# The output projection of an attention layer in fp16 parts, with half of its tiles moved into and behind the attention's units

## What is computed

```python
x = x + attention(layernorm(x))          # w_q, w_k, w_v, softmax(q k^T / 4) v, then w_o
x = x + ffn(layernorm(x))

def ffn(x):
    xq = int4_quant(x)                   # round(x*sqrt7/mean|x|), clipped to -8..7
    gate = bitlinear(xq, w_gate)         # weights rounded to -1, 0, 1 by their mean |w|
    up = bitlinear(xq, w_up)
    inter = int8_quant(up * relu(gate)**2)
    return bitlinear(inter, w_down)      # 512 -> 1376 -> 512
```

## Time and profile before

| | us |
|---|---|
| median of 3 runs (967.86 to 973.85) | 969.07 |
| the profiled execution, its time | 970.29 |
| its span, first to last instruction | 968.5 |
| PE busy / DVE busy / ACT busy / POOL busy in it | 919.0 / 851.1 / 772.3 / 140.1 |

### The profile page before, as it was taken

One profiled execution on the slowest core, in us unless ns is written; L12 is line 12 of the kernel. 1 busy time (PEld: TensorE's weight loads), 2 busy tenths in 40 slices (PEclk: granted clock), 3 DMA queues, 4 the chain that ended last, 5 costly groups with the idle time before them and its releaser, 6 DMA issues.

```text
span 968.5 us, 16815 instructions
## 1 busy us (share of the span) xinstructions
PE 919.0 (95%) x5934; PEld 300.9 (31%) x5934; DVE 851.1 (88%) x1513; ACT 772.3 (80%) x1437; POOL 140.1 (14%) x286
## 2 busy tenths in 40 slices
PE   4898999999999999999999999999898999999985
PEld 3333222222222222222222222222112245555542
DVE  7898899999999999999999999999877177877773
ACT  5653498999899998899998999898785877777773
POOL 3411011121111211112111121110002011112100
PEclk9999999999999999999999999999788999999997
DMA  9720021021121113102112111316540033111000
GB/s 353 228 90 1 0 71 41 24 56 51 50 56 40 40 35 80 41 23 57 54 47 55 40 42 37 78 40 178 185 104 12 12 130 111 45 44 55 22 24 32
DMA packets 38010, 64.92 MB, mean 67 GB/s; under 512 B 3622, under 2 KB 18982, under 8 KB 37670
## 3 DMA queue, kind: packets, MB, share of 16 engines
q1 hardware_dynamic: 37926, 63.85, 22.3%
HBM read 42.27 MB, written 21.23 MB: 66 GB/s over the span
## 4 chain that ended last, share of the span: by engine, by line
PE 80%; DVE 5%; ACT 4%; issue 2%; DMA 1%; SPq 1%; POOL 0%; ACTq 0%; POOLq 0%; DVEq 0%
PE ps L410 25%; PE ps L390 14%; PE ps L354 13%; PE ps L332 8%; PE ps L580 6%; PE ps L549 6%; PE ps L605 3%; DVE mx L1007 3%; PE ps L296 2%; DMA qk<-att_d 1%; ACT PB L744 1%; PE ps L371 1%; PE ps L595 1%; DVE hm L1103 1%; ACT XV L804 1%
## 5 line engine op out<-in xcount | busy, mean ns | idle before, releaser
L1007 DVE TENSOR_REDUCE mx<-ps 128x1 f32<-128x512 f32 x1024 | 632.5, 683 | 24.5 <-PE ps L354 18.1
L744 ACT ACTIVATE PB<-ps 128x512 f32<-128x512 f32 x1024 | 542.7, 597 | 77.0 <-PE ps L390 76.3
L354 PE MATMUL ps<-QK 48*128 48x512 f16 x1024 | 306.1, 388 | 9.3 <-DVE mx L1007 5.3
L390 PE MATMUL ps<-QK 50*128 50x512 f16 x1024 | 297.1, 388 | 3.5 <-ACT PB L744 2.5
L410 PE MATMUL ps<-PB,Vg 128*32 128x512 f32 x2048 | 278.1, 616 | 0.2 <-ACT PB L744 0.2
L390 PEld LDWEIGHTS ps<-QK 50*128 50x128 f16 x1024 | 70.9, 94 | 205.1 <-ACT PB L744 166.6
L354 PEld LDWEIGHTS ps<-QK 48*128 48x128 f16 x1024 | 76.0, 94 | 181.7 <-DVE mx L1007 152.2
L332 PE MATMUL ps<-XV,wqk 128*128 128x512 f16 x384 | 102.5, 385 | 0.0
L1282 POOL TENSOR_SCALAR nmb<-nm 128x16 f16<-128x16 f32 x32 | 6.5, 203 | 543.5 <-DVE nm L1012 543.5
L549 PE MATMUL ps<-wo,XV 128*128 128x512 f32 x128 | 63.1, 621 | 3.0 <-POOL XV L1327 3.0
L410 PEld LDWEIGHTS ps<-PB,Vg 128*32 128x32 f32 x2048 | 40.6, 108 | 69.6 <-ACT PB L744 36.8
(11 more groups left out here) (133 smaller groups left out, 652.6 us busy)
## 6 DMA issues: line engine op xcount, KB each, us to landing
parts_d<-spl SPq DMA_DIRECT2D x64, 128.0 KB
att_d<-OS SPq DMA_DIRECT2D x32, 256.0 KB
QK<-parts_d SPq DMA_DIRECT2D x48, 128.0 KB, 3.9
QK<-parts_d SPq DMA_DIRECT2D x16, 256.0 KB, 4.5
XV<-att_d SPq DMA_DIRECT2D x2, 2048.0 KB, 12.0
wqk<-x SPq DMA_DIRECT2D x16, 256.0 KB, 3.6
QK<-rden_d SPq DMA_DIRECT2D x8, 512.0 KB, 7.9
out<-PB SPq DMA_DIRECT2D x16, 256.0 KB, 2.0
```

The source lines that it names most:

```text
L354: nc.tensor.matmul(ps[:, at % S_BANKS, :], QK[rows, sup % 2, 2 * set_ + p, 0, half * HALF + qt * P:half * HALF + (qt + 1) * P], QK[rows, s ...
L390: nc.tensor.matmul(ps[:, T_BANK + n % T_BANKS, :], QK[rows, sup % 2, 2 * set_ + p, 1, kt * P:(kt + 1) * P], QK[rows, sup % 2, 2 * set_ + p ...
L744: nc.scalar.activation(PB[:, at % 3, i, :], ps[:, T_BANK + n % T_BANKS, :], ACT.Exp, scale=exp_reg).then_inc(probs, 1)
L1007: nc.vector.tensor_reduce(mx[:, v % 2, idx, kh:kh + 1], ps[:, at % S_BANKS, :], AX.X, ALU.max).then_inc(s_used, 1)
```

## The change

The output projection is done in fp16 parts: w_o is scaled by a power of two and split in a high and a low fp16 part, and so is the quotient `att`; a tile is then 12 fp16 matmuls (high x high, high x low, low x high, for four blocks of 128 channels) in place of 4 fp32 ones. Its weight parts lie in `wo`, its raw weights in the not yet used space of the down weights `td`.

- Tiles 0 to 3 are projected in units 26 to 29, in the places of a job. ACT copies the sum with its scale (`act_out_copy`), and POOL adds x (`pool_residual`). Tiles 4 to 7 are projected in the ramp, three matmuls in each step. Tiles 8 to 15 stay in the tail, in the same places (`pe_tile` 4 to 11); tiles 0 to 3 of the tail carry none.
- `pool_att` becomes three operations: product in fp32, cast, difference.
- Added inside the attention: denominators in and w_o in at unit 18 (SP), reciprocals of batch 0 at unit 19 (DVE; before: unit 28), quotients in at units 20 to 23 (SP; before: units 27 and 29), sum of squares of w_o at unit 20 (ACT), its spread over partitions, root and scales at unit 21 (PE, POOL, DVE), high part at unit 22 (ACT), low part at unit 23 (DVE).
- The down weights come in at units 27 and 28, their absolute sums are after steps 2, 10, 17 and 20 of the last super, the mean at step 22, and the rounding after the first two tiles' quantisation, in the ramp.
- The first gate and up chunk of tile 0 stands ahead of the last values' matmul. The scale of the value copies is a constant (two small DVE operations less at the start).

The core of the diff:

```diff
-            if step == RAMP:
-                pe.wait_ge(s_used, SUP_ITEMS * SUPERS)
-                pe_mean(pe, 2)
-            pe_attention_out(pe, (step - RAMP) // 4, step % 4)
             pe_scoresT(pe, sup, step, 0)
             pe_scoresT(pe, sup, step, 1)
             pe_av(pe, sup * STEPS + step - 2)
...
             pe_scoresT(pe, sup, step, 2)
             pe_scoresT(pe, sup, step, 3)
-            if step == 25:
+            if step == RAMP:
+                pe.wait_ge(s_used, SUP_ITEMS * SUPERS)
+            if step == RAMP + 6:
+                pe_mean(pe, 2)
+            n = step - RAMP
+            for m in range(3):
+                pe_attention_out(pe, UNIT_TILES + n // 4, n % 4 * 3 + m)
+            if step == RAMP + 9:
                 pe_xq_transpose(pe, 0)
...
                 def job(*pieces):
-                    if job_in(at):
-                        for m in pieces:
+                    for m in pieces:
+                        if job_in(at):
                             pe_job(pe, job_in(at), m)
+                        elif at >= FIRST_OUT:
+                            pe_attention_out(pe, at - FIRST_OUT, m)
...
                     scores(9)
+                    if at == 21:
+                        pe_norm(pe, 3)
                     if at + 1 < UNITS:
                         pe_max_rows(pe, at + 1)
...
+        def pe_attention_out(pe, t, m):
+
+            k, (a, b) = m // 3, PRODUCTS[m % 3]
+            if m == 0:
                 pe.wait_ge(att_ready, t + 1)
                 if t == 0:
-                    pe.wait_ge(wo_in, 64)
-                elif t == 1:
-                    pe.wait_ge(w_fac, 3)
-                elif t == 3:
+                    pe.wait_ge(wo_low, 1)
+                if t < UNIT_TILES:
+                    pe.wait_ge(rows_used, FIRST_OUT + t + 2)
+                elif t == BT - 1:
                     pe.wait_ge(xq_copy_dve, 1)
-                else:
-                    pe.wait_ge(x2_ready, t - 1 if t <= O_AHEAD else t)
-            last = nc.tensor.matmul(ps[:, o_bank(t), :], att[:, t % 2, g, :], wo[:, g, :],
-                                    start=(g == 0), stop=(g == SPB - 1))
-            if g == SPB - 1:
+                elif t >= UNIT_TILES + 2:
+                    pe.wait_ge(x2_ready, t - UNIT_TILES - (1 if t <= BT else 0))
+            last = nc.tensor.matmul(ps[:, o_bank(t), :], att[:, t % 2, a, k * P:(k + 1) * P], wop[:, b, k, :],
+                                    start=(m == 0), stop=(m == 3 * KT - 1))
...
+                if (at, r) == (20, 4):
+                    act_squares(act, 3)
+                if (at, r) == (22, 4):
+                    act_weights(act, 3, 0, HID)
+                if last and step in (2, 10, 17, 20):
+                    act_abs_down(act, (2, 10, 17, 20).index(step))
...
-                if n == (SUPERS - 1) * SUP_ITEMS + AHEAD + 7:
+                if n == 19 * UNIT_ITEMS + AHEAD + 16:
                     dve_reciprocal(dve, 0)
+                elif n == 21 * UNIT_ITEMS + AHEAD + 9:
+                    dve_total_squares(dve, 3)
+                elif n == 21 * UNIT_ITEMS + AHEAD + 22:
+                    dve_scales(dve, 3)
+                    dve_out_scale(dve)
+                elif n == 23 * UNIT_ITEMS + AHEAD + 4:
+                    dve_weights(dve, 3, 0, HID, 6)
...
         def pool_att(pool, t):
...
-            nc.gpsimd.tensor_tensor(att[:, t % 2, :, :], num[b][:, :, at:at + P], rdn[:, b, :, at:at + P], ALU.mult)\
-                .then_inc(att_ready, 1)
+            w = att32[b]
+            nc.gpsimd.tensor_tensor(w.rearrange("p (g t) -> p g t", g=SPB), num[b][:, :, at:at + P], rdn[b][:, :, at:at + P], ALU.mult)\
+                .then_inc(att_step, 1)
+            own_wait(pool, att_step, 2 * t + 1)
+            cast(att[:, t % 2, 0, :], w).then_inc(att_step, 1)
+            own_wait(pool, att_step, 2 * t + 2)
+            nc.gpsimd.tensor_tensor(att[:, t % 2, 1, :], w, att[:, t % 2, 0, :], ALU.subtract).then_inc(att_ready, 1)
```

More of the change, by code:

```diff
@@ L570, in pe_gate_up @@
                     pe.wait_ge(x2_ready, 2)
-                    for w in range(3):
+                    for w in range(2):
                         pe.wait_ge(w_tern[w], 4)
+                    pe.wait_ge(probs, 4 * UNITS * KEYT - 2)
                 else:
@@ L620, in pe_tile @@
                 pe_xq_transpose(pe, t + 1)
-            if t + O_AHEAD < TILES:
-                for g in range(SPB):
-                    pe_attention_out(pe, t + O_AHEAD, g)
+            if BT <= t + O_AHEAD < TILES:
+                for m in range(3 * KT):
+                    pe_attention_out(pe, t + O_AHEAD, m)
             if t >= 1:
@@ L719, in act_abs, with act_abs_down, act_out_copy @@
         def act_abs(act, w, q):
-            if wsum_first(w, q):
-                act.wait_ge(raw_in[w // 2], 16 * (4 + w // 2))
-                if w == 2:
-                    act.wait_ge(down_zero, 1)
+            if wsum_first(w, q) and w == 0:
+                act.wait_ge(gate_in, 16 * 4)
             nc.scalar.activation(ternq(w, q), raw(w, q), ACT.Abs, accum_out=wsum[:, w, q:q + 1]).then_inc(w_abs[w], 1)
+        def act_abs_down(act, q):
+            act.wait_ge(down_in[q // 2], (32, 48)[q // 2])
+            if q == 0:
+                for r in range(2):
+                    act.wait_ge(parts_out[r], 32 * 2 * SUPERS)
+            else:
+                act.wait_ge(w_abs[2], q)
+            if q == 2:
+                act.wait_ge(down_zero, 1)
+            nc.scalar.activation(spl[:, :, :, :].rearrange("p s a n -> p (s a n)").bitcast(BF16)[:, 0:DQ], raw(2, q), ACT.Abs,
+                                 accum_out=wsum[:, 2, q:q + 1]).then_inc(w_abs[2], 1)
+        def act_out_copy(act, t):
+            act.wait_ge(o_psum, t + 1)
+            if t == 0:
+                act.wait_ge(os_ready, 1)
+                act.wait_ge(job_split, JOBS)
+            elif t >= 2:
+                act.wait_ge(x2_pool, t - 1)
+            nc.scalar.activation(qk32[:, t % 2, :], ps[:, o_bank(t), :], ACT.Copy, scale=oscale[:, 1:2]).then_inc(o_copy, 1)
         def act_sign(act, w, q, order):
@@ L769, in act_superunit @@
                         act_rows(act, at + 1)
-                if last and step in (4, 6, 8, 10):
-                    act_abs(act, 2, (step - 4) // 2)
+                if (at, r) == (20, 4):
[4 more added lines that the diff above has]
+                    act_abs_down(act, (2, 10, 17, 20).index(step))
             if last:
@@ L1148, in dve_early_tiles @@
                     dve_quant(dve, 0)
+            dve_x2(dve, UNIT_TILES)
+            dve_total(dve, 2)
+            dve_factor(dve, 2)
+            for q in range(4):
+                dve_round(dve, 2, q, q)
+                if q == 3:
+                    dve.wait_ge(att_ready, BT)
+                dve_ternary(dve, 2, q, q)
+            nc.vector.tensor_scalar(wfd[:], wfac[:, 2:3], 1.0 / 127.0, None, ALU.mult)
             dve_xq_copy(dve, 0)
-            dve_x2(dve, 2)
-            dve_x2(dve, 3)
+            for t in range(UNIT_TILES + 1, BT):
+                dve_x2(dve, t)
         def dve_tile(dve, t):
```

261 lines of the change are left out of this document (154 added, 107 removed).

## The result

The changed kernel takes 956.96 us, the median of four runs (955.78 to 960.85), where the kernel before took 968.47 beside it (965.51 to 973.85): a ratio of 0.9882, 95% interval 0.9848 to 0.9917, so 1.2% faster, 11.5 us between the medians. In a later set of six runs it took 955.78 (953.36 to 958.41) against 969.71, a recorded ratio of 0.9839, interval 0.981 to 0.9869, and 13.9 us between the medians. One of the 17 runs of the kernel before in that set took 2120.3 us and doesn't count in the ratio. The profiled run of the first set is its slowest, 960.85 us with a span of 959.1; its stretches are cut at the places where the earlier trace rows cut those of before.

What follows compares the result with a forecast made beforehand. PE was taken to bound units with a job, DVE those without, 0.16 us apart. Costs of 8.1, 3.4 and 0.6 and gains of 10.2, 10.6, 0.6 and 10.0 sum to -19.3 from 970.3: 951 us, range 943 to 962.

Steps and rivals of the forecast that it cites:

- Inserted in units 19 to 23, 8.1 + 3.4: Units 19 to 23: moved reciprocals and w_o preparation cost 8.1 us, one 6.83 us stretch of half clock another 3.4.
- Units 26 and 27, +0.6: Units 26 and 27: becoming job units costs 2 x 0.16 us, the first quotient's close timing 0.3.
- rival D: Units 26 to 31: quotients or factors come late and PE stands, 1.5 us in unit 26, up to 5 in ramp; 957, chance 0.12.
- Units 28 and 29, -10.2: Mark of unit 28 to last joining: 44.91 us falls to 33.49 plus 1.2, without reciprocals or clock falls.
- two absolute sums behind which PE, now full, waits 0.6 each: Units 28 and 29: PE's waits behind ACT's sums of the down weights add 1.2 us.
- The ramp, -10.6: Ramp: 3.7 us gap and half clock (3.4) go, fp16 matmuls save 5.0, less 1.5 for ACT; step 2.70 to 2.39.
- the first chunk, -0.6: End of the ramp: tile 0's earlier gate and up chunk fills the wait for the last exponentials, saving 0.6 us.
- The tail, -10.0: Tail, maximum 0 to 15: 158.0 us against 167.98; projection tiles 10.46 in place of 11.37.
- the reciprocals of batch 1 stay there: Start of the tail: the first two tiles take 22.0 us, against 22.72 before.
- clock 1.00 from unit 26 on: From unit 26 on: a sign to look for, full granted clock of 1.00.
- A: Units 19 to 23: no clock fall (-3.4 us), banks hide more, insertions cost 5.5; 945, chance 0.18.
- B: Tail: POOL slows one DVE operation by 1.1 us in each of eight projection tiles, +8.9 us; 960, chance 0.10.

Runs made afterwards that it cites:

- experiment 8: Changed kernel with the four absolute sums of the down weights on DVE behind the first two tiles' moments instead of on ACT; median 953.84 us.
- experiment 1: Changed kernel with w_o's high part (ACT) and low part (DVE) each cut into four pieces; median 955.23 us.
- experiment 4: Changed kernel with w_o's squares, high part and low part over 8 columns in place of 512, the rest left out; median 949.83 us.
- experiment 3: Changed kernel with each of ACT's four absolute sums of the down weights over 64 columns in place of 1408; median 954.49 us.
- experiment 10: Kernel before the change with unit 28's batch 0 reciprocals over 8 of 256 columns; median 967.05 us against 969.71, ratio 0.997.
- experiment 2: Changed kernel without eleven of the twelve projection matmuls of each of the four tiles in units 26 to 29; median 957.29 us.
- experiment 11: Changed kernel with the batch 0 reciprocals made a second time, in unit 28, result unused; median 956.98 us.
- experiment 6: Changed kernel with tile 0's first gate and up chunk back behind the last attention matmuls; median 958.69 us.
- experiment 7: Changed kernel with ACT's first gate ahead of the copy of the last sums, and batch 1's reciprocal at the end of tile 1; median 957.76 us.
- experiment 5: Changed kernel without the third of the three fp16 products in the ramp and the tail; median 953.26 us.
- 9: Changed kernel with w_o's parts in pieces, absolute sums on DVE and first chunk back behind the last attention matmuls; median 952.13 us, ratio to before 0.9803.

## Why the prediction was right, and where its sizes were off

It said 951 within 943 to 962, and faster by over 1%; 956.96 it was. The gains and costs lie in the places that it named, but the sum was too good: it promised 19.3 us, and the spans of the two profiles differ by 9.4, the medians by 11.5 and 13.9. That the time came within 6.0 of 951 owes something to the reckoning from a profiled run of 970.3 where the median beside the changed kernel was 968.47: from that median the same sum would have given 949. Of the 9.9 us between the sum and the profiled run, 4.3 are the clock at its start, 2.8 the ramp, 1.6 the tail, 0.9 units 28 and 29, and 0.6 less 0.3 the rest.

*Inserted in units 19 to 23, 8.1 + 3.4.* Measured 12.1, with one fall of 6.83 as assumed, but the closeness is partly luck. Nine profiles with these operations whole hold 11.2 to 14.4, with 3.4 to 10.2 us of half clock. Two terms were off and cancelled: without any fall the insertions cost 9.7, not 8.1 (65.52 from mark 19 to 22 in the changed kernel and 44.62 from 22 to 24 in experiment 8, less five plain units), and the fall cost 2.4, not 3.4 (experiment 1). The squares were the worst-sized, 1.7 for 1.1: without them the distance of marks 20 to 21 goes from 23.20 to 21.52 (experiment 4). The fall stands behind the long wait for the low part in eight of nine profiles, and in none of the two with the parts in pieces.

*Units 26 and 27, +0.6.* Measured 0.3; no first matmul waited on POOL (rival D), though the first quotient's last part ended at 659.31, only 0.4 us ahead of the first matmul (659.74).

*Units 28 and 29, -10.2.* Measured -9.3. The step that was mis-sized is "two absolute sums behind which PE, now full, waits 0.6 each": 1.0 each (experiment 3). The excess before was shared out wrongly as well, 8.5 to the clock, 2.2 to the reciprocals and 0.7 to the sums; experiment 10 has at most 6.1 of clock, and 3.2 in PE's waits behind the sums. Half clock costs less than a mean clock says: the fall of 6.83 us between the marks of units 22 and 24 cost 2.4. And the reason "since the projection's matmuls fill PE" carries less than I gave it: without them the stretch was 0.5 longer (experiment 2). With the long wait back and PE full it kept its clock as well (experiment 11), so each of the two, no long wait or a full PE, kept most of the gain in one profile. But gaps and a long wait together don't always bring the falls of before either: experiment 10 had both, with 1.65 us in place of 2.19, and none until 720.2. What brought them stays open.

*The ramp, -10.6, and the first chunk, -0.6.* Together -11.2, measured -8.4 (58.08 to 49.63): the largest error in the terms. The gap and the half clock went, and the step of 2.39 came, as said. The "two absolute sums" with ACT's nearness were put at 1.5 and cost 2.0. The first chunk failed in sign, "it fills the wait for the last exponentials": ACT's gate was queued behind the copy of the last sums, so the chunk's 1.27 us (776.40 to 777.67) only moved the last attention matmuls, +0.8 by experiment 6. The rest, about 0.8, was not tested. Part of the half clock had lain in the gap that I counted apart (it began at 729.6, the first projection at 730.66, so 0.5 was counted twice), and PE's mean, in the gap before, now stands in a step. DVE's rounding was in time, its last operation at 764.91.

*The tail, -10.0.* Measured -8.4. The pitch was right twice (10.47 for 10.46, 10.40 for 10.39). Mis-sized is "the reciprocals of batch 1 stay there" at 22.0 for two tiles: 22.49, since a projection no longer covers them and the loop pays them whole (experiment 7). And tile 12 to 13, without a projection, had a fall, 11.18 for 10.39, as in five of the twelve profiles of the changed kernel and its versions. With that a sign of the prediction failed, "clock 1.00 from unit 26 on": the clock was 1.00 up to the ramp's end, and three falls of 3.4 us lie in the tail (0.97). Another sign held in part: units 20, 21 and 22 took 3.1, 0.7 and 4.8 us more, not 1 to 3.

*Not separated.* No run makes the projection in fp32 in its new places. That the fp16 parts give 5.0 in the ramp and 7.2 in the tail (16 x 0.31, 8 x 0.90) is reckoned from lengths and pitches, which came out as forecast, and not from a run without them.

*Rivals.* A's 945 would have needed full clock in units 19 to 23 and insertions at 5.5; without a fall they cost 9.7. B: beside a quotient of POOL's DVE's clipping takes 1.21 us, and 0.43 without one.

```profile
855.24 1.27 POOL L1421 TENSOR_TENSOR XV<-XV,QK 128x512 f32<-128x512 f32 x1
...
855.58 1.21 DVE L1147 TENSOR_SCALAR qk<-QK 128x512 bf16<-128x512 f32 x1
...
782.23 0.43 DVE L1147 TENSOR_SCALAR qk<-QK 128x512 bf16<-128x512 f32 x1
```

The mechanism is there, and costs nothing: the tile's pitch stays 10.47, and 10.40 in experiment 5, where PE is not the limit. The Trainium skill, SBUF — State Buffer, section "Who interferes with whom", lets such an operation and GpSimd shut each other out of a port pair; by that rule the trace agrees in the lengths, while the loop had the room. C, half clock behind every insertion, came in part: one to three falls in units 20 to 23 where the operations are whole, none in the ramp of any version of the changed kernel.

## What to carry to other kernels

Before an operation is put into a full stretch, cut it in pieces: the wait behind it shortens (1.8 us here), and half clock behind it may go too (2.4 us in the stretch of one profile, not seen in the median); its own time is paid either way. Look for the engine that is idle near that stretch: four sums cost 4.0 us on ACT and 0.3 on DVE, a few places later in the program. And when a chunk is moved ahead to fill a gap, read the queue of the engine that consumes it; if that engine is parked on a later event, the chunk fills nothing. And before a gain is read from one profile, look where its run stands among the others: the profiled runs of experiments 1, 9 and 10 were the fastest of theirs, and their medians kept less than half of what the stretches gained.
